# Two stores moved to SP's queue, and GpSimd releasing the result buffers of a mixture-of-experts loop

## The reference

```python
# layer norm, rounding to 8 bits, one matmul with the rounded context
x = x + tanh(g_xattn) * (fake_quant(layernorm(x)) @ fake_quant(ctx))
# 8 experts, each row goes to its best 2
y      = layernorm(x)
logits = y @ W_gate + b_gate
top    = top_k(logits, 2)
y_all  = relu(einsum('bsd,edh->bseh', y, W_e) + b_e)
x = x + tanh(g_ffn) * y_all[top].mean(axis=2)
```

## Time and profile before

| | |
|---|---|
| median of 3 runs | 374.94 us (374.0 to 375.22) |
| the profiled execution's own time | 374.94 us |
| its span | 373.2 us |
| TensorE busy | 330.3 us, 89% |
| DVE busy | 227.3 us, 61% |
| ACT busy | 129.9 us, 35% |
| GpSimd (POOL) busy | 131.0 us, 35% |
| mean DMA rate | 218 GB/s |

### The profile page before, as it was taken

The page is one execution under the profiler, slowest core; times in us unless marked ns, Lnnn a source line. Parts: engine busy times, 40 slices in busy tenths (PEclk is TensorE's granted clock), DMA queues, the critical chain, the costliest instruction groups (busy, mean ns, idle before and its releaser), DMA issues.

```text
span 373.2 us, 6919 instructions
## 1 busy us (share of the span) xinstructions
PE 330.3 (89%) x1746; PEld 253.8 (68%) x1756; DVE 227.3 (61%) x321; ACT 129.9 (35%) x109; POOL 131.0 (35%) x138
## 2 busy tenths in 40 slices
PE   5669887999665899999999999999999999999950
PEld 1224364676552788888888888888888888888840
DVE  3898994858989884178858632943229433923320
ACT  3866865544101350175518112611117113511100
POOL 3652450300234333356334621943218431333210
PEclk9899998999758899999999999999999999999995
DMA  6999395411293999739999974796257963654233
GB/s 234 412 409 384 141 346 219 168 59 59 85 305 119 358 408 305 169 108 343 358 414 295 350 219 105 218 396 154 76 112 205 395 155 99 157 112 71 57 98 56
DMA packets 23004, 81.46 MB, mean 218 GB/s; under 512 B 3152, under 2 KB 3152, under 8 KB 22992
## 3 DMA queue, kind: packets, MB, share of 16 engines
q1 hardware_dynamic: 16368, 57.71, 41.0%
q0 software_dynamic: 6480, 23.60, 25.7%
q10 hardware_dynamic: 144, 0.01, 0.0%
HBM read 62.43 MB, written 18.87 MB: 218 GB/s over the span
## 4 chain that ended last, share of the span: by engine, by line
PE 64%; DVE 2%; DVEq 0%; issue 0%; POOL 0%; POOLq 0%
PE ps L1197 59%; PE ps_y L1174 5%; DVE w_lo L929 1%; POOL out_dram L469 0%; DVE res L960 0%; DVE yT_lo L923 0%; DVEq L267 0%; DVE res L962 0%; DVEq L275 0%; DVEq L960 0%; POOLq L268 0%; DVEq L268 0%; DVE tab L917 0%; DVEq L270 0%; DVEq L962 0%
## 5 line engine op out<-in xcount | busy, mean ns | idle before, releaser
L1197 PE MATMUL ps<-w_hi,yT_hi 128*128 x320 | 101.2, 397 | 4.5 <-DVE yT_lo L923 4.5
L1197 PE MATMUL ps<-w_lo,yT_hi 128*128 x320 | 99.2, 391 | 0.0
L1197 PE MATMUL ps<-w_hi,yT_lo 128*128 x320 | 99.1, 391 | 0.0
L469 POOL DMA_INDIRECT out_dram<-res,sidx x20 | 38.3, 1914 | 123.4 <-DVE res L962 115.3
L929 DVE TENSOR_TENSOR w_lo<-stage,w_hi 128x2048 f32 (+1 forms) x32 | 72.2, 2288 | 10.3 <-ACT w_hi L613 8.8
L613 ACT ACTIVATE w_hi<-stage 128x2048 f32 x28 | 52.5, 1913 | 56.5 <-PE ps L1197 43.1
L960 DVE TENSOR_TENSOR res<-ps,bias 128x1024 f32<-128x1024 f32 x20 | 24.5, 1223 | 75.7 <-PE ps L1197 73.9
L1197 PEld LDWEIGHTS ps<-w_hi,yT_hi 128*128 128x128 f32 x320 | 59.0, 190 | 15.7 <-issue 4.7
L1197 PEld LDWEIGHTS ps<-w_hi,yT_lo 128*128 128x128 f32 x320 | 60.4, 189 | 12.8
L1197 PEld LDWEIGHTS ps<-w_lo,yT_hi 128*128 128x128 f32 x320 | 60.4, 189 | 12.8
L599 ACT ACTIVATE yT_hi<-ps_y 128x1024 fp32r<-128x1024 f32 x21 | 21.5, 1026 | 126.6 <-PE ps_y L1174 126.6
(11 more groups left out here) (157 smaller groups left out, 272.7 us busy)
## 6 DMA issues: line engine op xcount, KB each, us to landing
stage<-in_L_ffn_W_e_dram SPq DMA_DIRECT2D x32, 1024.0 KB, 8.5
stage<-in_ctx_dram SPq DMA_DIRECT2D x16, 512.0 KB, 11.4
xt<-in_x_dram SPq DMA_DIRECT2D x8, 512.0 KB, 11.2
y_scratch<-y SPq DMA_DIRECT2D x8, 512.0 KB, 3.2
bias<-in_L_ffn_b_e_dram SPq DMA_DIRECT2D x8, 512.0 KB, 4.4
out_dram<-xt SPq DMA_DIRECT2D x6, 512.0 KB, 2.9
out_dram<-xt POOLq DMA_DIRECT2D x2, 512.0 KB, 7.7
y_rows<-y_scratch,gidx POOLq DMA_INDIRECT x22, 6.2
```

What stands on the lines that cost most here:

```text
L469: pool.indirect_dma_start(out=out_rows[:, :], out_offset=bass.IndirectOffsetOnAxis(ap=sidx[:, q:q + 1], axis=0), in_=res[q][:, :], in_offs ...
L1197: last = pe.matmul(ps[q][:, h * 512:(h + 1) * 512], lhs[q][:, k, :], w[:, bass.ds(woff + k * D + h * 512, 512)], start=(k == 0 and lhs is ...
```

## The change

Three things change. The x_new stores of tiles 6 and 7 go from GpSimd's queue to SP's, so all eight count on `s_oi`. A new semaphore, `s_resf`, says which result buffers are free; DVE waits on it in place of `s_sc`. And GpSimd, which counts it up, now waits at the end of each step until the scatter that it has just issued has landed; the wait for the scatter before, ahead of the next scatter, is gone.

```diff
@@ SP
-            for i in range(TPB, NT - 2):
+            for i in range(TPB, NT):
                 store_x_new(i)
@@ GpSimd, before its slot loop
-            for i in (NT - 2, NT - 1):
-                pool.wait_ge(s_oa, i + 1)
-                pool.dma_start(out_t[i], xt[:, i, :]).then_inc(s_sc, 16)
...
-            pool.wait_ge(s_oi, 16 * (NT - 2))
-            pool.wait_ge(s_sc, 32)
+            pool.wait_ge(s_oi, 16 * NT)
+            pool.sem_inc(s_resf, 2)
@@ GpSimd, step
                 pool.wait_ge(s_pool, slot * 2 + 4)
-                pool.wait_ge(s_sc, slot * 16 + 32)
-                settle(pool)
                 pool.wait_ge(s_post, slot + 1)
                 settle(pool)
                 pool.indirect_dma_start(out=out_rows[:, :], ... , compute_op=ALU.add).then_inc(s_sc, 16)
+                pool.wait_ge(s_sc, slot * 16 + 16)
+                pool.sem_inc(s_resf, 1)
...
-            pool.wait_ge(s_sc, n * 16 + 32)
+            pool.wait_ge(s_sc, n * 16)
@@ ACT and DVE, before their slot loops
-            wait_ge(s_oi, 16 * (NT - 2))
-            wait_ge(s_sc, 32)
+            wait_ge(s_oi, 16 * NT)
@@ DVE, step
-                dve.wait_ge(s_sc, slot * 16 + 16)
+                dve.wait_ge(s_resf, slot + 1)
```

More of the change, by code:

```diff
@@ L218, in flamingo_gated_moe @@
         s_post = sem("slot_result_ready")
+        s_resf = sem("slot_result_free")
         s_sc = sem("slot_scattered")
@@ L603, in _ @@
             evacuate_hi(0, 0)
-            act.wait_ge(s_oi, 16 * (NT - 2))
-            act.wait_ge(s_sc, 32)
+            act.wait_ge(s_oi, 16 * NT)
             def step(slot, q, turn):
@@ L937, in _ @@
                 split_lo(c, c + 1, slice(c * CW, (c + 1) * CW))
-            dve.wait_ge(s_oi, 16 * (NT - 2))
-            dve.wait_ge(s_sc, 32)
+            dve.wait_ge(s_oi, 16 * NT)
             def step(slot, q, turn):
```

## The result

| | before | changed |
|---|---|---|
| median | 374.47 us (4 runs) | 394.61 us (4 runs) |
| span of the profiled execution | 373.2 us | 394.9 us |

The ratio is 1.054, 95% interval 1.047 to 1.061: 20 us slower. Of seven executions of the changed kernel, two (399.40, one of the four above, and 399.46) are over 1.5% above the fastest and count as slow; the ratio is of fast ones alone, and the five others have a median of 394.0. The forecast was 393.5, in a range of 377 to 404.

The account below looks back on a forecast made before the run. TensorE bounds the kernel before; GpSimd's closed round would bind after. 19 rounds of 10.8 plus 32.6 us put the last scatter 18.7 us later: 374.94 + 18.7 = 393.6, said as 393.5, range 377 to 404.

Parts of the forecast that it names:

- Parts 1 and 2: Two stores moved to SP's queue, and DVE waiting on s_resf instead of s_sc: 0 each.
- One sign: Expected in the trace: up to 140 us nothing moves by more than 0.5.
- Part 3: GpSimd waits for its own scatter, with the next gather queued behind: last scatter 18.7 us later.
- The quiet round: GpSimd's loop from scatter to scatter without loads or splits: 10.8 us, hidden under TensorE's 11.79.
- The loaded part: GpSimd's rounds during weight loads and splits: 15.6 us each when loaded, 32.6 us more in all.
- The reserve of 4 us: Slot 4's gather lands 4 us before TensorE needs it; slack gone after one or two loaded rounds, near 185.
- TensorE 12.7 us late: TensorE's delay by slot 19, whose gather lands at 351.6 and was needed at 338.9.
- The rounds fit: Rival: loaded scatters land in 6 to 7 us without the gather, rounds stay near 12; 375 us, chance 0.14.
- Half the load: Rival: landings of about 8 us or fewer meetings with splits, loaded rounds of 13.2; 381 us, chance 0.22.

Follow-up runs that it names:

- run 1: The kernel before with only the x_new stores moved to SP's queue, two 4 KB scratch copies replacing them on GpSimd's: 375.27 us, ratio 1.0008.
- run 3: The changed kernel with the wait for the landing and the count on s_resf moved behind the next gather and second copy: 375.32 us, ratio 1.0006.
- run 2: The kernel before with only GpSimd's wait moved to its own scatter's landing at the step's end: 397.22 us, ratio 1.059.
- run 7: The changed kernel with one more 128 x 1 copy on GpSimd, waited for, behind the wait for the landing: 410.75 us, ratio 1.092.
- run 9: The changed kernel with GpSimd's loop of slots cut from 12 turns to the 10 this input uses: 391.97 us, ratio 1.041.
- run 5: The changed kernel with SP's weight loads of experts 1 to 7 cut to an eighth: 376.12 us, ratio 1.0034.
- run 6: The changed kernel with DVE's splits of experts 2 to 7 cut to 128 of 2048 columns a chunk: 378.98 us, ratio 1.008.
- run 4: The changed kernel with the landing wait moved behind the next gather's table read and copy, ahead of its issue: 375.63 us, ratio 1.0043.

## Why the prediction was right, step by step

**Parts 1 and 2 cost nothing.** Right (runs 1 and 3). One sign failed: nothing was to move by more than 0.5 us before 140, but in the profiled execution of the changed kernel the transpose inside slot 1 starts 0.97 later (139.25 and 138.28 in TensorE's order of time). 0.46 of that is a later first product (122.74 and 122.28); the rest is the granted clock, which stayed at 0.50 (1.2 GHz) until 126 there and until 125 before. In run 1, which has the same stores on SP, the same transpose starts at 137.00, so this is no cost of part 1.

**Part 3 is a closed round through landing, gather and scatter.** Right: run 2 has all of the loss, run 3 has none of it, and run 7 gets longer with the round, in its quiet slots by 0.4 each.

**The quiet round, 10.8 us.** Slightly too long. The eight rounds under 11 us have a mean of 10.5. The scatter lands in 6.0 to 6.4 instead of 5.8, but the second copy starts at once behind the gather (287.48 = 286.48 + 1.00, where 1.7 was reckoned).

**The loaded part, 32.6 us more.** Mis-sized: 238.8 - 19 x 10.5 = 39.3. The other eleven rounds took 11.5 to 18.6 us. Most of the excess is the landings: in these eleven rounds they sum to 95.1 us, 27 more than eleven quiet ones of 6.2, where the forecast had 3.0 more in six rounds, 18. The four slowest are 10.7 to 11.2, where 8.8 was taken. Part of that is the issue, which a landing includes: five of 20 issues of the scatter took 2.7 us or longer, three before. Why GpSimd's work met the splits more often was not tried; that it now stands at another place in the slot is the likely reason. The two errors, -5.7 and +6.7, nearly cancel: the last scatter was forecast at 381.7 and came at 383.08. So the total is better than its terms, and that is luck.

**The reserve of 4 us, gone near 185; TensorE 12.7 us late.** The first gap ends at 190.03. The gaps sum to 13.3, but the last product ends 16.5 us later than before (the transpose inside slot 19 starts at 367.04 in TensorE's order of time, before at 350.5). Most of the difference is the 0.97 ahead of slot 1's transpose and the 1.9 by which the slots behind the first three gaps were longer, below. The last result then waits 4.4 for GpSimd (378.66 to 383.08), where 6 was forecast.

**The end.** Left out: the skipped slots, 1.3 to 1.5 us (run 9). The profiled execution's 396.6 us are thus the 393.6 reckoned, 0.4 at the start, 1.0 in the rounds and 1.6 at the end; that the median, 394.61, lies closer to the forecast is luck again.

**The rivals.** *The rounds fit* rested on landings that would be short without the gather beside them; six were 9.1 to 11.2 in the loads. *Half the load* is what runs 5 and 6 made by hand, and they came out below its 381 (its own terms give 380: 143.86 + 205.2 + 19 is 5.1 behind 362.98). What I had wrong there is how the two loads combine. By the medians, small loads leave 0.8 us of the loss (1.3 by the ratio), small splits 3.7 (3.0), and both whole 20. They don't add. My reading, which no run tests by itself, is that every quiet slot forgives 1.3 us and the reserve another 4, and what is over that falls through whole.

The page "DMA: Bandwidth & Descriptors" of the Trainium skill, section on the anatomy of a DMA, would give 3.2 us for each landing by an estimate; no landing of the scatter took under 5.8 in any run, so the trace doesn't bear it out for this scatter with addition. As to "SBUF — State Buffer" of the Trainium skill, section "Who interferes with whom": with the splits whole, issues of the scatter took up to 3.09 us, and up to 3.52 with small loads (run 5); with small splits none took over 1.62 (run 6). So here the splits, DVE's instructions with two SBUF inputs, do hold the issue up, which the page infers they would not.

## What to carry to other kernels

A wait on an engine that is mostly idle is not free if a prefetch is queued behind it: add up the whole round from landing to landing, in quiet and in loaded stretches, and compare it with the slot of the engine that sets the pace. If quiet rounds leave room, a loaded one may be late; moving the wait behind the prefetch (run 3) was worth all 20 us, and moving it by 2 us of work (run 4) nearly all. And put no wait ahead of loop turns that are only skipped.

## What the runs showed of the hardware that was not expected

A gap of 7.1 us in TensorE's work cost more than the gap. The stretch 218 to 223 and the next (the last three numbers: granted clock, DMA share, GB/s):
```profile
218.00:223.00 5.00, 0.32 (x2) 0.32 (x3) 0.00 (x0) 0.00 (x0) 0.09 (x1) 0.59 1.01 323
223.00:229.00 6.00, 6.00 (x26) 5.16 (x25) 1.22 (x1) 1.02 (x1) 1.23 (x3) 0.78 0.25 50
```
The granted clock was 0.59 on average over these 5 us of the gap and 0.78 over the next 6: in slices of 1 us it was 0.94 in the one from 218, after TensorE had stopped at 215.6, then 0.50 (1.2 GHz) up to 225, and 1.00 (2.4 GHz) from 226. The slot behind the gap took 235.94 - 222.68 = 13.3 us instead of 11.79: 1.5 lost. The shorter gaps, of 1.5 and 3.5 us, left slots of 12.0 us behind them, without their own gaps (203.58 - 1.54 - 190.03, 222.68 - 7.10 - 203.58), 0.2 each. Here the granted clock was 1.00 all through, and the engine was no slower: most of the 0.2 is how a gap is counted. In the stream an entry of two products is 0.62 long and the next starts 0.46 after it, so a gap counted from the end of the last one leaves out 0.16.
